# Attention on one core: scores and maxima dealt out in six rounds of two row tiles, the product with V in half sets, and a shorter way in

## The reference, cut to what matters

```python
qkv = (tokens @ w_proj + b_proj).reshape(B, N, NUM_HEADS, 3 * HEAD_DIM)   # N = 1024, 8 heads of 16
q, k, v = jnp.split(qkv, 3, axis=-1)
attn = jnp.einsum('bihd,bjhd->bijh', q, k) * SCALE
attn = jax.nn.softmax(attn, axis=2)
res = jnp.einsum('bijh,bjhd->bihd', attn, v).reshape(B, N, NUM_HEADS * HEAD_DIM)
out = res @ w_out + b_out + tokens
```

## Time and profile before

| | us |
|---|---|
| median of 3 runs | 1369.55 (1369.17 to 1369.75) |
| the profiled execution | 1369.05 |
| its span | 1367.3 |
| ahead of the first score | 84 |
| from there to the first score of the last step | 776 |
| from there to the last instruction of the attention | 51.3 |
| spiking attention, routing, experts, result | 456 |

### The profile page before, as it was taken

The page is one execution under the profiler, slowest core; times in us unless marked ns, Lnnn a source line. Parts: engine busy times, 40 slices in busy tenths (PEclk is TensorE's granted clock), DMA queues, the critical chain, the costliest instruction groups (busy, mean ns, idle before and its releaser), DMA issues. The chain is left out here.

```text
span 1367.3 us, 20269 instructions
## 1 busy us (share of the span) xinstructions
PE 1145.2 (84%) x6982; PEld 515.2 (38%) x6982; DVE 923.2 (68%) x1619; ACT 741.6 (54%) x1525; POOL 283.0 (21%) x345
## 2 busy tenths in 40 slices
PE   2479999999999999999999999858758555999933
PEld 1012232232232232232223222225447255999922
DVE  3779878877877877877877887027874764555523
ACT  1037777777777777777777777841112112555512
POOL 2031021022022012013013000005300566000766
PEclk8569999999999999999999999989975766999966
DMA  3903533533533533534523520027000012222414
GB/s 91 160 19 82 96 64 82 97 62 82 97 63 82 97 62 83 98 50 94 97 46 83 98 40 8 17 81 216 0 1 0 33 43 80 67 66 64 121 56 151
DMA packets 72301, 100.05 MB, mean 73 GB/s; under 512 B 15888, under 2 KB 53136, under 8 KB 67600
## 3 DMA queue, kind: packets, MB, share of 16 engines
q1 hardware_dynamic: 68112, 90.44, 31.6%
q0 software_dynamic: 4096, 8.40, 2.0%
HBM read 67.27 MB, written 31.26 MB: 72 GB/s over the span
## 5 line engine op out<-in xcount | busy, mean ns | idle before, releaser
L533 DVE TENSOR_REDUCE neg_max<-slot 128x1 f32<-128x1024 f32 x512 | 605.7, 1220 | 135.6 <-PE slot L396 130.4
L467 ACT ACTIVATE probs<-ring 128x512 f32<-128x512 f32 x1024 | 557.5, 601 | 203.8 <-PE ring L386 198.5
L386 PE MATMUL ring<-stack 98*128 98x512 bf16 x1024 | 347.1, 387 | 11.4 <-ACT probs L467 7.3
L366 PE MATMUL acc<-probs,v_sb 128*32 128x512 f32 x2048 | 272.7, 605 | 0.1
L396 PE MATMUL slot<-twin_k,twin_q 48*128 48x512 bf16 x1024 | 207.1, 401 | 49.0 <-DMA twin_k<-parts_dram 27.7
L386 PEld LDWEIGHTS ring<-stack 98*128 98x128 bf16 x1024 | 80.7, 96 | 253.7 <-issue 186.3
L396 PEld LDWEIGHTS slot<-twin_k,twin_q 48*128 48x128 bf16 x1024 | 49.4, 93 | 293.4 <-issue 174.9
L1174 ACT ACTIVATE hid_t<-ps_h,b_of 128x128 f32<-128x128 f32 x312 | 88.9, 367 | 74.9 <-PE ps_h L1133 74.9
L336 POOL CAST m_parts<-neg_max 128x32 bf16<-128x32 f32 x16 | 3.4, 210 | 589.5 <-issue 499.3
L1244 POOL DMA_INDIRECT z_all<-rows_out,pos_out x64 | 70.6, 1103 | 127.1 <-SPq L1099 102.0
L1133 PE MATMUL ps_h<-xt,w_of 128*128 128x128 f32 x624 | 86.0, 282 | 7.8 <-DVE xt L1203 7.8
(11 more groups left out here) (139 smaller groups left out, 1026.0 us busy)
## 6 DMA issues: line engine op xcount, KB each, us to landing
parts_dram<-parts SPq DMA_DIRECT2D x32, 384.0 KB, 5.4
stack<-parts_dram SPq DMA_DIRECT2D x32, 384.0 KB, 6.7
twin_q<-parts_dram SPq DMA_DIRECT2D x32, 256.0 KB, 8.1
stack<-parts_dram SPq DMA_DIRECT2D x32, 256.0 KB, 8.3
rows_in<-zeros SPq DMA_DIRECT2D x1, 5056.0 KB, 19.8
x_in<-rows_in SPq DMA_DIRECT2D x79, 64.0 KB
rows_out<-y SPq DMA_DIRECT2D x78, 64.0 KB
xp<-in_x SPq DMA_DIRECT2D x8, 512.0 KB, 10.6
```

The lines of the kernel that those rows point to most:

```text
L366: mm = pe.matmul(acc[32 * h:32 * h + 32, :], v_sb[s // G % 2][:, kt, s % G * HG + h, :], probs[:, j % PROBS, h, :], start=(kt == 0), stop= ...
L386: pe.matmul(out[:, :], stack[1][s % G][0:KROWS + MROWS, h, kt * P:(kt + 1) * P], stack[0][s % G][0:KROWS + MROWS, h, half * HALF:(half + 1 ...
L467: act.activation(probs[:, j % PROBS, i % HG, :], ps[:, :], ACT.Exp).then_inc(emptied, 1)
L533: dve.tensor_reduce(neg_max[u % 2][:, k:k + 1], ps[:, :], AX.X, ALU.max, negate=True).then_inc(emptied, 1)
```

## The change

The maxima and scores share the array in two **row tiles**: rows 0 to 63 (tile 0) and 64 to 127 (tile 1). A score becomes two matmuls: 50 rows at row 0 (the first run of parts and the two rows of the maximum, `start`), then 48 rows at row 64 (the other two runs, `stop`), both into the same bank; the second waits until the first is complete (`s_begun`). A maximum becomes two halves of 512 keys with a bank each, one in each tile, each reduced by itself (`neg_half`), and one operation on VectorE joins the halves of 16 maxima (`least`). A **block** is one group of four scores with two maxima: six rounds, in each of which one matmul goes to tile 0 and one to tile 1 (`ROUNDS`; 0 to 3 are the scores, 4 and 5 the maxima). One half of a V set (256 of 512 columns) stands behind the third round, the other behind the sixth; the first and the last set of each accumulation go whole. Side jobs stand behind the second half set.

PSUM is dealt out anew: 4 banks `ring`, 3 banks `slot`, `acc`. V and the output move from `slot` to `ring` and from VectorE to ScalarE; their biases are folded into one vector that GpSimd adds to the residual (`b_sum`). Maximum rows are handed over every 16 maxima instead of every 32 (`mturn`), and only 22 maxima stand ahead of the first block. The maxima then run 22 to 26 ahead.

At the start the weights are loaded first and rearranged by ScalarE instead of VectorE, ScalarE makes the first part of each projection of image 0, and SyncE stores and loads what the first maxima need as soon as three of four projections are split, with the query half loaded from ScalarE's queue. Q parts are loaded in halves of 512 queries. In the steps the parts of the next image are stored, and its stack loaded, ahead of the load of the residual (`xr`); there are 3 stacks instead of 2.

```diff
 PARTS = 3
-RUNS = [(0, 0, 3), (0, 1, 2), (0, 2, 1)]
-KROWS = DH * sum(n for _, _, n in RUNS)
+RUN_A = (0, 0, 3)
+RUNS_B = [(0, 1, 2), (0, 2, 1)]
+A, BB = 0, 64
+RUN_ROWS = DH * 3
 MROWS = 2
 
-S_BANKS, M_SLOTS = 3, 2
-S_KINDS = ("score", "proj", "back", "mturn")
-M_KINDS = ("max", "v", "oturn", "out")
-PV_LAG = 7
-COPY_AT = (35, 3)
-EARLY, LANE = 7, 41
+STEPS = UNITS = B * G
+QB = HG * KT // 2
...
+STACK_DMAS, TWIN_DMAS = 9, 6
+LEAD_DMAS = 4
+
+BLOCKS = 2 * KT
+
+S_BANKS, M_BANKS = 4, 3
+S_KINDS = ("score", "proj", "v", "bias", "back", "mturn", "out")
+M_KINDS = ("max", "oturn")
 PROBS = 4
-
-
-def vector_lane(s):
+COPY_AT = (KT + 1, 1)
+AHEAD_FIRST, AHEAD_MAX = 22, 26
+OUTS = 4
...
+ROUNDS = ((0, 4), (1, 5), (2, 0), (3, 1), (4, 2), (5, 3))
+
+
+def side_jobs(s):
 
     b, g = s // G, s % G
-    lane = []
-    if s + 1 < STEPS:
-        first = EARLY if s else 0
-        lane += [((n - first) * 50 / (KT * HG - first), 1.15, "max", (s + 1, n)) for n in range(first, KT * HG)]
-    if s + 2 < STEPS:
-        lane += [(51 + 1.8 * n, 1.15, "max", (s + 2, n)) for n in range(EARLY)]
+    jobs = [(10, "oturn", (s, 0))]
     if s:
-        lane.append((8, 0.8, "oturn", (s - 1, 1)))
-    lane.append((42, 0.8, "oturn", (s, 0)))
-    if g == 0 and s:
-        lane += [(20, 0.7, "out", (b - 1, 1)), (22, 0.8, "stats", (b - 1, 1)), (24, 0.3, "aggr", (b - 1, 1))]
-    if g == 1:
-        lane += [(54, 0.7, "out", (b, 0)), (56, 0.8, "stats", (b, 0)), (58, 0.3, "aggr", (b, 0))]
+        jobs.append((2, "oturn", (s - 1, 1)))
+    for n in (0, 1):
+        q = 2 * s + 1 + n
+        if q < 2 * UNITS:
+            jobs.append((5 if q == 1 else 4 + 8 * n, "mturn", (q,)))
+    if g == 0:
         if b + 1 < B:
-            lane.append((30, 1.2, "v", (b + 1,)))
-    lane.sort(key=lambda j: j[0])
-    total, so_far, out = max(LANE, sum(j[1] for j in lane)), 0, []
-    for want, weight, kind, args in lane:
-        out.append((want if s + 1 == STEPS else ITEMS * so_far / total, kind, args))
-        so_far += weight
-    return out
+            jobs += [(at, "proj", (b + 1, n)) for n, at in enumerate((0, 1, 3, 5))]
+        if b:
+            jobs += [(6, "back", (b - 1, 1)), (8, "out", (b - 1, 2)), (9, "out", (b - 1, 3))]
+        else:
+            jobs.append((7, "bias", ()))
+    else:
+        if b + 1 < B:
+            jobs += [(6, "v", (b + 1, 0)), (8, "v", (b + 1, 1))]
+        jobs += [(13, "back", (b, 0)), (14, "out", (b, 0)), (15, "out", (b, 1))]
+    return jobs
...
+    m = AHEAD_FIRST
+    for t in range(STEPS * BLOCKS):
+        maxima = min(2, 2 * UNITS * QB - m)
+        put(10 * t, "block", (t // BLOCKS, t % BLOCKS, m, maxima))
+        put(10 * t + 2, "rest", (t // BLOCKS, t % BLOCKS, m, maxima))
+        if t % KT in (0, KT - 1):
+            put(10 * t + (21 if t % KT else 23), "pv", (t // BLOCKS, t % BLOCKS, 0, 2))
+        else:
+            for part in range(2):
+                put(10 * t + 21 + 2 * part, "pv", (t // BLOCKS, t % BLOCKS, part, 1))
+        m += maxima
+        if t % 2 and m < 2 * t + 2 + AHEAD_MAX and maxima:
+            for n in range(2):
+                put(10 * t + 7, "solo", (m + n,))
+            m += 2
...
+        for at, kind, args in side_jobs(s):
+            t = s * BLOCKS + at
...
+    first = [("proj", (0, n)) for n in range(4)] + [("v", (0, n)) for n in range(2)]
+    first += [("solo", (n,)) for n in range(QB + 1)] + [("mturn", (0,))]
+    first += [("solo", (n,)) for n in range(QB + 1, AHEAD_FIRST)]
...
+def halves(job):
+
+
+    kind, args = job
+    if kind == "solo":
+        return [(("max", (args[0], tile)), tile, 1) for tile in range(2)]
+    if kind not in ("block", "rest"):
+        return []
+    s, j, m, maxima = args
+    met, out = set(), []
+    for r, pair in enumerate(ROUNDS):
+        for tile, n in enumerate(pair):
+            use = ("score", (s, 4 * j + n)) if n < HG else ("max", (m + n - HG, tile))
+            if n < HG + maxima and (kind == "rest") == (r >= len(ROUNDS) // 2):
+                out.append((use, tile, int(n >= HG or use in met)))
+            met.add(use)
+    return out
...
-            put_parts(0)
-            load_twins(0)
-            load_stack(0)
-            load_twins(1)
+            sp.dma_start(w_o[:, :], w_out).then_inc(s_wo, 16)
...
+            sp.wait_ge(s_early, 6)
+            put(0, 1, 0, 1, 2, slice(0, N), s_put[0])
+            put(0, 0, 0, 0, 2, slice(0, HALF), s_put[0])
+            sp.wait_ge(s_put[0], 16 * PUT_DMAS[0])
+            load_k(sp, stack_k[0], 0, 0, RUNS_AT_B, s_lead)
+            load_k(sp, twin_k[0], 0, 0, RUNS_TWIN, s_lead, HALF)
+
+            sp.wait_ge(s_early, 8)
+            put(0, 0, 0, 0, 2, slice(HALF, N), s_put[1])
+            sp.wait_ge(s_split, 4)
+            put(0, 1, 0, 0, 1, slice(0, N), s_put[1])
+            put(0, 0, 0, 2, 1, slice(0, N), s_put[1])
+            sp.wait_ge(s_put[1], 16 * PUT_DMAS[1])
+            load_q(sp, stack_q[0], 0, 0, RUNS_AT_B, (1,), s_stack[0])
+            load_q(sp, twin_q[0], 0, 0, RUNS_TWIN, (1,), s_twin[0])
+            sp.wait_ge(s_ones, 1)
+            load_k(sp, stack_k[0], 0, 0, RUNS_AT_A, s_stack[0])
+            load_q(sp, stack_q[0], 0, 0, RUNS_AT_A, (0, 1), s_stack[0])
+            for s in (1, 0):
+                put(0, s, 1, 0, PARTS, slice(0, N), s_put[2])
+            sp.wait_ge(s_put[2], 16 * PUT_DMAS[2])
             load_stack(1)
-            sp.dma_start(w_o[:, :], w_out).then_inc(s_wo, 16)
-                if g == 0:
+            load_twin(1)
+            for b in range(B):
+                put_max_rows(4 * b + 1)
+                if b + 1 < B:
+                    put_parts(b + 1)
+                    load_stack(2 * b + 2)
+                put_max_rows(4 * b + 2)
+                if b:
+                    wait_filled(sp, ("out", (b - 1, OUTS - 1)))
+                sp.dma_start(xr[:, :], x[b]).then_inc(s_xr, 16)
+                if b + 1 < B:
+                    load_twin(2 * b + 2)
                     if b + 2 < B:
-                        wait_filled(sp, ("v", (b,)))
+                        wait_filled(sp, ("v", (b, 1)))
                         sp.dma_start(xp[b % 2][:, :], x[b + 2]).then_inc(s_x[b % 2], 16)
-                    if b + 1 < B:
-                        put_parts(b + 1)
-                else:
-                    if b:
-                        wait_filled(sp, ("out", (b - 1, 1)))
-                    sp.dma_start(xr[:, :], x[b]).then_inc(s_xr, 16)
-                if s + 2 < STEPS:
-                    wait_filled(sp, ("max", (s, KT * HG - 1)))
-                    load_twins(s + 2)
-                if s + 1 < STEPS:
-                    put_max_rows(s + 1)
+                    load_stack(2 * b + 3)
+                put_max_rows(4 * b + 3)
+                if b + 1 < B:
+                    load_twin(2 * b + 3)
+                    put_max_rows(4 * b + 4)
 
...
+            def score(out, s, i, base, start):
+                j, h = i // HG, i % HG
+                half, kt = j // KT, j % KT
+                rows = slice(base, base + RUN_ROWS + (MROWS if base == A else 0))
+                return pe.matmul(out[:, :], stack_k[s % STACK_BUFS][rows, h, kt * P:(kt + 1) * P],
...
+                    kind, args = use
+                    if kind == "max":
+                        unit_ready(args[0] // QB, args[0] % QB)
+                        maximum(free_bank(use), *args).then_inc(m_fill[tile], 1)
+                    elif not last:
+                        score(free_bank(use), *args, (A, BB)[tile], True).then_inc(s_begun[tile], 1)
+                        begun[tile] += 1
+                        first[use] = s_begun[tile], begun[tile]
+                    else:
+                        pe.wait_ge(*first[use])
+                        out = ring[S_USE[use] % S_BANKS]
+                        score(out, *args, (A, BB)[tile], False).then_inc(s_fill[tile], 1)
+
+            def pv(s, j, part, count):
+                half, kt = j // KT, j % KT
...
+                if q >= 2 and k == 0:
+                    dve.wait_ge(s_mp, q - 1)
+                wait_filled(dve, use)
+                dve.tensor_reduce(neg_half[q % 2][:, half, k:k + 1], slot[n % M_BANKS][:, :], AX.X, ALU.max,
+                                  negate=True).then_inc(m_empty[n % M_BANKS], 1)
+
+            def least(q):
+                for use in last_maxima(q):
+                    wait_taken(dve, use)
+                dve.tensor_tensor(neg_max[q % 2][:, :], neg_half[q % 2][:, 0, :], neg_half[q % 2][:, 1, :],
+                                  ALU.min).then_inc(s_least, 1)
...
```

680 lines of the change are left out of this document (389 added, 291 removed).

## The result

The changed kernel takes 1329.08 us (median of 4 runs, 1326.02 to 1330.03), the kernel before 1369.65 us beside it (4 runs, 1369.17 to 1374.59): a ratio of 0.9692 with a 95% interval of 0.9664 to 0.972, faster by 3.1%. The forecast was 1324. The profiled execution took 1328.38 us, with a span of 1326.6 against 1367.3.

What follows compares the result with a forecast made beforehand. TensorE was taken to bound each step at 51.7 us. The terms -31 (way in), -20 (fifteen steps) and +6 us (last step) make -45 from 1369, so 1324 us; range 1298 to 1354.

Steps and rivals of the forecast that it cites:

- The way in: Stretch to the first score: first maximum near 26 us, first score at 53 instead of 84, so -31 us.
- The other path: Start: 16 maxima end at 45.5 us, then 4.0 from GpSimd taking the last to the first score: 49.5, against 53.
- (a): Second half of a score waits for the first: 0.43 us, just hidden by two rounds of 0.44.
- Rival 2: In each block's third and sixth round the second half's wait shows; from 0.09 us each the change no longer pays; 6%.
- (b): ScalarE's copy of acc delays three exponentials and TensorE waits: up to 0.9 us, twice a step, taken as 1.2 a step.
- (c): VectorE's half reductions, 0.69 us alone, 0.60 in a row: 42 to 48 us a step, not the bound; 0.4 added.
- Fifteen steps: The first fifteen attention steps: 50.4 us each against 51.7, 756 against 776 in all, so -20 us.
- Transfers: Stack and twin loads issued 7 blocks (20 us) ahead, maximum rows four blocks (11 us) ahead: costed at nothing.
- rival 1: Rounds run as costed, but ScalarE's and VectorE's waits keep a step at 51.7 us: 1344 us; chance 20%.
- (3): Rival: weight loads or the change of tile show, 0.1 us in each of 1536 rounds: +154, near 1478 us; 4%.
- rival 4: Waits in the steps shrink to at most 0.5 us a step: another -17 to -20, 1305 us; chance 17%.
- (5): Rival: loads come late at each step's start, up to 3 us, since Q parts move in 1 KB pieces: 1344 to 1369; 6%.

Runs made afterwards that it cites:

- e4: Changed kernel with all parts of the first image stored in one batch once everything is split: 1427.08 us, ratio 0.9804 to the kernel before on a slower chip.
- e12: Changed kernel with 32 maxima ahead of the first score instead of 22, and AHEAD_MAX 36 instead of 26: 1417.5 us, ratio 1.0344 to the kernel before.
- e11: Changed kernel with all eight loads for the first maxima issued by SyncE, none on ScalarE's queue: 1329.76 us, ratio 0.9684 to the kernel before.
- e9: Changed kernel with VectorE reducing only the first 256 keys of each half maximum of 512: 1321.56 us, ratio 0.9629 to the kernel before.
- e3: Changed kernel with second halves of each block's first two scores one round behind their first halves, not two: 1461.6 us, ratio 1.0041 on a slower chip.
- e1: Changed kernel with ScalarE's copy of acc behind the fourth exponential of its block instead of the first: 1415.2 us, ratio 0.9735 on a slower chip.
- e6: Changed kernel with each accumulation's last V set behind the sixth round instead of the third, and acc copied behind the fourth exponential: 1316.67 us, ratio 0.96.
- e8: Changed kernel with inner V sets whole behind the third round instead of in halves: 1357.25 us, ratio 0.9904 to the kernel before.
- e5: Changed kernel run again unedited, on the chip of later variants: 1327.25 us, ratio 0.9682 to the kernel before.
- e7: Changed kernel with every V set whole behind the sixth round and acc copied behind the fourth exponential: 1293.41 us, ratio 0.9427 to the kernel before.

## Why the prediction was right, and where it was not

**The way in** (-31 predicted, -32.8 measured). Right in its terms: weights first and ScalarE in VectorE's place bring the first projection 5.9 us forward; the order of stores is worth 8.2 to 9.7 (e4); ten maxima fewer 12 (e12). The term for two queues, in which four issues each stood in for eight in a row, is nothing by itself (e11). The other path was underrated: put at 49.5 with a first maximum at 26, it was to be 3.5 us shorter than VectorE's. In e9 it is 0.4 shorter, 25.8 us from the first maximum, since its rows wait for SyncE. That 48.6 stands near 49.5 is luck. What of the remaining 5 to 7 us is fewer issues and what is fewer bytes was not tried.

**The block** (2.66 and 2.42 predicted, 2.67 and 2.42 measured). Right. The unit prices read from the kernel before, 0.22 a stream and 0.10 a change of division, carried over to an order of instructions that it did not have. The rule of the Trainium skill that was weighed (TensorE: Matmul & The Clock Gate, Part 3, The mechanism) would have put 0.107 us on every round, if one goes by its list of what overlaps; the text above that list also lets a load into a background weight buffer go ahead. Rounds at 0.216 to 0.227 us, weight loads of the same rows included, speak against the list here.

**(a) The wait of the second half.** Costed at nothing, and nothing shows. But the sum behind it was 0.43 against 0.44, and where the wait does show the second half starts 0.446 to 0.448 us behind the first (e3), against two rounds and a stagger of 0.446 to 0.447: the release takes up to 0.06 to 0.07 where 0.04 was counted. That the cover held is in part luck. Rival 2 did not come, but its deciding point of 0.09 us per wait is less than half of what one round less costs (0.22, e3). The semaphore tail of the same page of the Trainium skill (87 ns behind a pair) would have shown by some 0.03 us and did not.

**(b) ScalarE's copy.** The size was right (up to 0.9 predicted, 0.93 measured in odd steps), the mechanism wrong. The step that failed: "ScalarE copies `acc` out behind the first exponential ... and has a whole V set to wait for there; the next three exponentials are late by about that". Moving the copy gains nothing (e1). A whole set behind the third round keeps TensorE from finishing the second, third and fourth score for 1.0 us and ScalarE runs dry. It then works off what is left at 0.48 to 0.49 us an exponential, and the next block's second to fourth round come at that pace (0.49) instead of 0.22, since each needs the bank of one of them. Behind the sixth round four finished scores stand ready when the set starts. With the last sets there, 10 us come back (e6), 0.7 a step where the term was 1.2; with the inner ones put whole behind the third round it costs 28 (e8).

**(c) VectorE.** 0.69 alone and 0.60 in a row: measured 0.684 and 0.60. Not the bound of steps 1 to 14 (e9), as said.

**Fifteen steps** (-20 predicted, -12.6 measured). This is the term that was mis-sized, and the main reason why the forecast is 5 us below the measurement. Predicted 756, measured 764.0: 2.8 us from steps 1 to 14 (50.6 each against 50.4) and 5.2 from step 0, costed like any other at 50.4, which took 55.6. The mean of 51.7 from which it started hid the same thing: before, step 0 took 54.4 at a granted clock of 0.95 and the others 51.6 at 1.00. So steps 1 to 14 gained 1.0 us each, and step 0 lost 1.2.

Two things make step 0 long, and the traces do not part them fully. One is the clock. These are step 0 in e5 (the same program as the changed kernel), in e11 (which differs ahead of the step alone) and in e9:

```profile
50.20:104.80 54.60, 51.98 (x417) 16.99 (x416) 46.82 (x79) 37.19 (x71) 15.80 (x21) 0.93 0.39 82
48.70:106.90 58.20, 56.36 (x419) 17.76 (x419) 46.88 (x79) 37.29 (x71) 15.47 (x21) 0.84 0.36 74
48.60:99.30 50.70, 49.38 (x418) 16.58 (x420) 27.87 (x76) 37.08 (x71) 15.94 (x21) 0.96 0.42 83
```

The changed kernel has 55.6 us at 0.91. In e5 the clock is at its half level for 8.0 us of the step, in the changed kernel for 9.8, in e11 for 18.5: 10.5 us more at that level make the step 3.6 longer. The changed kernel against e5 is 1.8 us more and 1.0 longer. By these, an estimate, the 9.8 us cost 3 to 5 of the 5.2. The other is VectorE: blocks 1 and 3 of step 0 have two further maxima each (`solo`), with no scores beside them, and TensorE waits there for slots. With the reductions cut, step 0 takes 50.6 (e9), but the clock is at half for only 3.8 us there, so the 5.0 us are not all VectorE's. In block 2, at the full clock in both, it is 3.71 against 2.84 us.

**The last step** (57.2 predicted, 56.6 measured, 58.2 in e5) and **everything behind** (0 predicted, -1.2): right. As predicted its blocks keep 2.67 us without maxima.

**Transfers.** Costed at nothing, and so they are: no idle time of TensorE between the first score and the last step is over 0.7 us, where e12's wait for loads is 7. But the reason was too generous: "a good 7 blocks (20 us)" is 14.65 us, and of it 6.9 are slack (e12). Transfers were not far from being the next bound.

**The rivals.** A step did not stay at 51.7 (1), rounds are packed (3), waits did not shrink (4), loads are not late (5). The sign given for rival 1, waits for banks of over 3 us a step, did come: weight loads wait 45.4 us for exponentials, 12.8 for the copies of projections (`full`) and 10.5 for slots from 107 to 815 us, 4.9 a step. It was a poor sign, since a weight load that waits need not hold up its matmul. But 1 and 4 both touched what was open: waits for ScalarE are there, and taking them away is worth more (33.8 us, e7) than rival 4 allowed (20), since half sets are given up with them.

**Where the expected gain of the half sets is.** Whole sets behind the third round 899.4, halves 871.2, whole sets behind the sixth 838.5 (attention's end, one chip). Halves cost TensorE 0.24 us a block and save it waits for ScalarE, compared with the first; compared with the last they only cost.

## What to carry to other kernels

When engines run nearly level (here 2.40 us of VectorE and 2.42 to 2.67 of TensorE a block, with 1.9 of ScalarE beside them), the order inside a block decides as much as the amounts: put a long run of work that feeds nobody where the engines behind have just been handed everything, not ahead of what they wait for. Unit prices per stream and per change of division can be read from pairs of starts and reused to 0.01 us; the first step, the granted clock in it, the margins of covers (here nothing that shows for a wait, 6.9 us for loads) and what an engine waits for need rows of their own. Before a difference in one stretch is put down to an edit, compare the granted clock of both. Test a cause by moving it alone: the size of a stall may be right while its name is wrong.

## What the runs showed of the hardware that was not expected

Matmuls that alternate between two row tiles run at 0.216 to 0.227 us for 512 columns, both tiles at once, with a weight load ahead of each and no visible cost for it. A matmul that waits for another one starts 0.446 to 0.448 us behind that matmul's start, 0.06 to 0.07 behind the end of its record (e3). Wherever TensorE stood idle for some 7 us in the steps of e12, the granted clock went to half for 6.8 to 13.7 us. On one chip (e1 to e4) everything behind the attention took 535 to 545 us instead of 455, with the attention's steps unchanged. Of it some 70 us are idle time of TensorE ahead of the experts' matmuls (L1378 in e1: weight loads wait 70.1 us, the longest 28.8; 2.1 us in e5); what ends it the profile does not name.
